# Two-layer MoE block on one core: SP's loads reordered, the first routing and its routed stage rescheduled, the low part of two slots on another engine

## The chip, the cores and the metric

One core of one Trainium2 chip. The metric is the device time of one launch in microseconds (us). The kernel before takes 1633.12 us, the median of three runs (1630.59 to 1636.07).

## What is computed

The reference takes x of 4 images of 512x512 and applies three residual steps:

```python
x = x + 0.5 * ffn(layernorm(x))      # mixture of experts
x = x + attn(layernorm(x))           # windowed attention, 16 channels
x = x + 0.5 * ffn(layernorm(x))      # the same mixture again

def ffn(x):
    shared = (silu(x @ sw1.T) * (x @ sw2.T)) @ sw3.T          # hidden 2048
    scores = sigmoid(x @ router_w.T)                          # 8 experts
    idx = top_k(scores + expert_bias, 2); w = scores[idx] / sum
    routed = sum over the two experts of w * expert(x)        # hidden 256 each
    return shared + routed
```

The attention looks at 8-token windows along rows for one half of the channels and along columns for the other, adds a depthwise convolution of v, projects, normalises and adds the residual.

## The kernel before

All five engines run programs written out by hand, synchronised by semaphores; each engine executes its own in order. Time is cut into *slots*. A slot is one 128-wide piece of the shared expert's hidden layer for one image of 512 rows: a gate product G and an up product U (12 matmuls each, L1253: each fp32 operand is split in a bf16 high and low part and three partial products are made), ScalarE's Silu of G (L1479), VectorE's multiply of U by it (L1634), ScalarE's bf16 high part of the result (L1489), the low part as fp32 minus high part (GpSimd, L1587), and the down product (12 matmuls, L1267) that accumulates in `psD`. TensorE does in slot s: G(s), U(s), then down(s-1). U(s) waits for the multiply of slot s-1, down(s-1) for the low part of slot s-1.

There are 128 slots: 16 for each image (UNIT), four images for the first mixture and four for the second. Around these, each engine's `slot(s)` fits in the rest of the work by tables:

- *Tiles* (`Prep`, 32): load 128 rows, statistics, norm (`vec_norm`, L382), store to `xnd`, transpose ("rows", L388), router logits (L408). `vec_norm` of tile n waits until the store of tile n-2 has landed.
- *Splits* (`SPLITS`): raw fp32 weights are loaded by SP (`load_raw`) and split into bf16 high (ScalarE, L257) and low (VectorE, L262) parts, eight shared chunks in slots -2 to 13 and eight experts after them. Shared chunks are stored and later reloaded by ScalarE's queue (`load_gu`, `load_down`).
- *Routing* (`route`, slots 14 to 17 for the first mixture): VectorE picks two experts of each token; TensorE computes the ranks (`pe_ranks`, L609) at position 3 of slot 15; lists of rows for each block are made in slots 18 and 19 (`vec_list`, `pe_list`, L639), indices in slot 21.
- *Constants of the attention*: loaded by ScalarE's queue from slot `CONST_SLOT` on; their product with the bias (`bias_product`) one slot ahead of `BIAS_SLOT`; VectorE does 18 small steps in slots `BIAS_SLOT` and the next three.
- *Routed stage* (`routed`): before slots `ROUTED_AT` = 24 and 116 every engine goes through 39 blocks of 128 gathered rows times the weights of one expert (L1355, L1372, L1385, L1397), about 187 us each. Slot 23's down product is flushed first. At its end GpSimd issues the gathers of the first three combine tiles, and then enters the slot.
- *Combine* (`Combine`, 16 tiles each time): GpSimd gathers two rows for each token (L555), SP loads the third (L561), VectorE sums (L576, L579), for the first four tiles it also makes statistics and norm (L591), SP stores (L567, L570). `COMBINE_SLOT` puts tiles 0, 1 in the slot behind the stage, then 2, then 3 and 4, then 5, then 6 and 7. Only then, in slots 35 to 39, tiles 8 to 15.
- *Halves* (`Half`, 8 units of the attention): SP loads a unit in 8 DMAs of 64 KB (`Half.sp_load`, L949), TensorE transposes it ("turn", L969, slots D-2) and projects it (L982), VectorE does softmax and products in pieces (`vec_work`, L1002, L1016, L1033) from slot D to slot B, then "back" and "proj" on TensorE, and in `NORM_SLOT` VectorE's `vec_spread` and `vec_finish` (L1112 to L1129), for which TensorE's "out" transposes wait (L1137). D is 29, 37, 46, 55, 64, 72, 81, 90. `spare` estimates the free VectorE time of a slot, and the pieces are put in by it.
- *Evacuations* (`Evac`): after 16 slots `psD` is added to the rows; image 1's first part is evacuated at the first routed stage (`EVACS`).

SP's order is what `slot(s)` in its block writes: prep loads, evacuation loads and stores, the combine's stores of this slot, the loads of the next slot's combine tiles, prep stores, weight stores and raw loads, then the units' loads. The first unit's load stands in slot 26 and the second's in slot 33.

## Time and profile before

| | us |
|---|---|
| median of three runs | 1633.12 |
| the profiled execution | 1636.73 |
| its span | 1634.7 |
| mean granted TensorE clock | 0.978 of full speed |

| engine | busy us | share |
|---|---|---|
| TensorE matmuls (PE) | 1536.6 | 94% |
| VectorE (DVE) | 997.5 | 61% |
| ScalarE (ACT) | 557.1 | 34% |
| GpSimd (POOL) | 503.6 | 31% |

The times are of one profiled execution. An engine's busy time counts only while it executes; waiting, and the issuing of a DMA, are idle. Idle time of an engine is listed with what ended it, for instance `[3.60 <-DVE rows L707]`: 3.60 us idle, ended by VectorE's instruction of line 707. "Granted clock" is the share of TensorE's full speed that the chip allowed (1.00 is 2.4 GHz, 0.50 is 1.2 GHz).

### The profile page before, as it was taken

How to read it: one execution, taken by the hardware profiler on the slowest of the kernel's cores; microseconds unless marked ns; L12 is line 12 of the kernel's file. 1: busy time of each engine (PE TensorE's matmuls, PEld its weight loads, DVE VectorE, ACT ScalarE, POOL GpSimd, SP SyncE). 2: the span in 40 equal slices, each digit the busy share in tenths (PEclk: the TensorE clock that was granted, in tenths of full speed). 3: DMA queues.
4: the chain of work that ended last, by engine and by line, in shares of the span. 5: the costliest groups of instructions: out<-in, count | busy, mean ns of one | idle time of the engine just before them, and what ended most of it. 6: DMA issues, size and time to landing. Idle time of an engine off the chain costs nothing.

```text
span 1634.7 us, 21706 instructions
## 1 busy us (share of the span) xinstructions
PE 1536.6 (94%) x7574; PEld 772.5 (47%) x7574; DVE 997.5 (61%) x1390; ACT 557.1 (34%) x1080; POOL 503.6 (31%) x424
## 2 busy tenths in 40 slices
PE   5999898999959798989998999999999999999999
PEld 3555344555424344535544554455445444555444
DVE  3665743444336788798779888888933543444333
ACT  3456222444312223333433433343322213444211
POOL 1321112222233555152434443252512112222253
PEclk9999999999979899999999999999999999999999
DMA  6887424333463675144423642264227234334485
GB/s 232 310 303 288 157 90 148 117 116 116 125 185 110 184 228 154 40 137 142 129 70 104 165 157 65 98 180 148 54 89 221 76 111 139 116 116 116 136 293 199
DMA packets 117465, 243.76 MB, mean 149 GB/s; under 512 B 15985, under 2 KB 40562, under 8 KB 113906
## 3 DMA queue, kind: packets, MB, share of 16 engines
q1 hardware_dynamic: 79632, 138.97, 25.1%
q10 hardware_dynamic: 26370, 66.17, 13.0%
q0 software_dynamic: 11360, 37.23, 7.8%
q8 instruction: 66, 1.08, 0.3%
q14 instruction: 37, 0.30, 0.1%
HBM read 168.39 MB, written 72.88 MB: 148 GB/s over the span
## 4 chain that ended last, share of the span: by engine, by line
PE 78%; DVE 11%; issue 4%; DMA 3%; POOL 1%; ACT 1%; SPq 1%; POOLq 0%; ACTq 0%; DVEq 0%
PE bank L1253 32%; PE bank L1267 15%; PE bank L1372 12%; PE bank L1397 6%; PE bank L982 3%; PE bank L1355 2%; DVE region L1002 2%; PE bank L1094 1%; PE bank L408 1%; PE bank L1385 1%; DMA rows<-sorted_y,slots 1%; DVE region L1016 1%; DVE stats L417 1%; PE bank L388 1%; DMA region<-xnd,idxs 1%
## 5 line engine op out<-in xcount | busy, mean ns | idle before, releaser
L1253 PE MATMUL bank<-xT,wb 128*128 128x512 bf16 x2688 | 620.2, 382 | 8.0 <-DVE wb L262 4.5
L1253 PEld LDWEIGHTS bank<-xT,wb 128*128 128x128 bf16 x2688 | 264.8, 99 | 322.1 <-issue 22.6
L1587 POOL TENSOR_TENSOR hs<-sgh,hs 128x512 bf16<-128x512 f32 x128 | 157.9, 1233 | 752.3 <-ACT hs L1489 752.2
L1267 PE MATMUL bank<-wb,hs 128*128 128x512 bf16 x1536 | 367.5, 384 | 4.2 <-POOL hs L1587 4.2
L1634 DVE TENSOR_TENSOR sgh<-bank,sgh 128x512 f32<-128x512 f32 x128 | 88.1, 688 | 274.5 <-PE bank L1253 273.5
L1267 PEld LDWEIGHTS bank<-wb,hs 128*128 128x128 bf16 x1536 | 151.4, 100 | 182.5 <-issue 12.0
L1372 PE MATMUL bank<-wr,region 128*128 x936 | 232.1, 385 | 0.0
L1489 ACT ACTIVATE hs<-sgh 128x512 bf16<-128x512 f32 x128 | 80.9, 632 | 331.0 <-DVE sgh L1634 327.1
L1002 DVE TENSOR_TENSOR region<-region 128x1024 f32<-128x1024 f32 x128 | 184.4, 1441 | 2.4
L1580 POOL DMA_INDIRECT region<-xnd,idxs x78 | 74.0, 949 | 257.5 <-PE bank L1355 256.0
L1479 ACT ACTIVATE sgh<-bank 128x512 f32<-128x512 f32 x128 | 76.3, 596 | 216.1 <-PE bank L1253 213.2
L1372 PEld LDWEIGHTS bank<-wr,region 128*128 128x128 bf16 x936 | 89.4, 99 | 78.9 <-issue 5.8
L1397 PE MATMUL bank<-wr,region 128*128 x468 | 113.7, 379 | 1.2 <-DVE region L1704 1.2
L1694 DVE TENSOR_TENSOR region<-bank,region 128x256 f32<-128x256 f32 x78 | 33.1, 424 | 105.6 <-ACT region L1521 105.6
L1687 DVE TENSOR_TENSOR region<-bank,region 128x512 bf16<-128x512 f32 x78 | 53.9, 691 | 58.4 <-ACT region L1515 58.2
L1521 ACT ACTIVATE region<-bank 128x256 f32<-128x256 f32 x78 | 29.9, 383 | 172.7 <-PE bank L1372 172.7
L555 POOL DMA_INDIRECT rows<-sorted_y,slots x64 | 64.9, 1014 | 74.1 <-issue 68.8
L1253 PE MATMUL bank<-region,wb 128*128 128x512 bf16 x384 | 85.3, 379 | 0.0
L1016 DVE TENSOR_REDUCE region<-region 128x128 f32<-128x1024 f32 x64 | 78.1, 1220 | 2.2
L1033 DVE TENSOR_REDUCE region<-region 128x128 f32<-128x1024 f32 x64 | 78.1, 1220 | 2.2
L1397 PEld LDWEIGHTS bank<-wr,region 128*128 128x128 bf16 x468 | 45.6, 98 | 56.3 <-issue 1.5
L576 DVE SCALAR_TENSOR_TENSOR rows<-rows,coef 128x512 f32<-128x512 f32 x32 | 29.5, 920 | 55.5 <-DMA rows<-x2p 32.2
(161 smaller groups left out, 1600.2 us busy)
## 6 DMA issues: line engine op xcount, KB each, us to landing
wb<-wsplit ACTq DMA_DIRECT2D x42, 1024.0 KB, 6.0
wb<-wsplit ACTq DMA_DIRECT2D x42, 512.0 KB, 4.0
sorted_y<-region SPq DMA_DIRECT2D x78, 256.0 KB, 2.0
wsplit<-wb SPq DMA_DIRECT2D x8, 1536.0 KB, 6.8
wr<-wall SPq DMA_DIRECT2D x6, 1536.0 KB, 7.7
rows<-x SPq DMA_DIRECT2D x32, 256.0 KB, 5.4
region<-wall SPq DMA_DIRECT2D x8, 1024.0 KB, 8.5
xnd<-rows SPq DMA_DIRECT2D x32, 256.0 KB, 2.8
```

The source lines that it names most:

```text
L1002: o.do(e.tensor_tensor(t, few.to_broadcast(full), many.to_broadcast(full), ALU.mult))
L1016: o.do(e.tensor_reduce(self.s[r][:, two], self.tmp.rearrange("p (n c) -> p n c", c=H), AX.X, ALU.add))
L1033: o.do(e.tensor_reduce(self.Q[r][:, two], self.tmp.rearrange("p (n b) -> p n b", b=WL), AX.X, ALU.add))
L1253: m = e.matmul(ps[:], wb[:, w % 2, wp, at:at + P], xt[:, xp, c, :], start=(i == 0), stop=(i == 3 * NDC - 1))
L1267: m = e.matmul(psD[tt][:], hs[:, s % 2, hp, tt * P:(tt + 1) * P], wb[:, w % 2, wp, at:at + D], start=(first and i == 0), stop=(last and i ...
L1372: m = e.matmul(psH[k % 2][:], xsT[k % 2][:, xp, c * P:(c + 1) * P], words_of(k, wp, c * D), start=(n == 0), stop=(n == 3 * NDC - 1))
L1397: m = e.matmul(psY[k % 2][:], hT[k % 2][:, hp, kt, :], words_of(k, wp, at), start=(n == 0), stop=(n == 3 * KT - 1))
L1479: e.activation(sgh[:, s % 2, :], psG[:], ACT.Silu).then_inc(S("h_silu").sem, 1)
L1489: e.activation(hs[:, s % 2, 0, :], sgh[:, s % 2, :], ACT.Copy).then_inc(S("h_hi").sem, 1)
L1580: e.indirect_dma_start(out=xs[k % RX], out_offset=None, in_=xnd, in_offset=bass.IndirectOffsetOnAxis(ap=idxs[:, k:k + 1], axis=0)).then_in ...
L1587: e.tensor_tensor(hs[:, s % 2, 1, :], sgh[:, s % 2, :], hs[:, s % 2, 0, :], ALU.subtract).then_inc(S("h_lo").sem, 1)
L1634: e.tensor_tensor(sgh[:, s % 2, :], psU[:], sgh[:, s % 2, :], ALU.mult).then_inc(S("h_mul").sem, 1)
```

## The change

- SP: expert 0's raw weights are loaded in the prologue behind the first two shared chunks, and experts 1 to 5 each two slots sooner; all experts' splits are two slots sooner, but the last's one slot later. The load of the first unit moves from slot 26 to slot 24, that of the second from slot 33 to slot 28.
- The first routed stage stands before slot 23 instead of 24. The combine tiles 0 to 7 and the evacuation at it move with it; `D_SLOT` stays.
- Constants are loaded one slot sooner, the bias product and VectorE's bias steps two slots sooner (slots 12 to 15). The first ranks product moves from slot 15, position 3 to slot 16, position 0.
- In slots 23 and 116 VectorE makes the low part, right behind its multiply, and GpSimd doesn't.
- `spare` takes 7.0 instead of 5.5 off a norm slot. Of the softmax pieces four move by it: half 4's `scores 1,1` from slot 66 to 65, half 5's `scores 1,0` from 74 to 75, half 7's `scores 1,2` from 92 to 93 and `values 0,0` from 93 to 94.

```diff
--- before.py
+++ after.py
@@ -83,7 +83,7 @@
     UNIT = NU * KT
     UNITS = 2 * IMAGES
     SLOTS_ALL = UNITS * UNIT
-    ROUTED_AT = (UNIT + 8, 7 * UNIT + 4)
+    ROUTED_AT = (UNIT + 7, 7 * UNIT + 4)
     assert W3OFF + KT * D == WW and NB == 39 and UNIT == 16 and NU == E and NT == 16
 
 
@@ -216,7 +216,7 @@
         for w in range(NU):
             SPLITS += [(2 * w - 2, "gu", w), (2 * w - 1, "down", w)]
         for ex in range(E):
-            at = 2 * ex + 4 if ex < E - 1 else UNIT + 3
+            at = 2 * ex + 2 if ex < E - 1 else UNIT + 4
             SPLITS += [(at, "gu", NU + ex), (at + 1, "down", NU + ex)]
         SPLITS.sort(key=lambda p: p[0])
         SPLIT_NO = {(kind, n): k for k, (_, kind, n) in enumerate(SPLITS)}
@@ -283,7 +283,7 @@
             if s % 2 == 0 and 0 <= s < 2 * (NU - 2):
                 return [s // 2 + 2]
             if s % 2 == 1 and 0 < s < 2 * (E - 2):
-                return [NU + s // 2]
+                return [NU + s // 2 + 1] if s // 2 + 1 < E - 2 else []
             return [NU + E - 2] if s == 2 * NU - 4 else [NU + E - 1] if s == 2 * NU - 2 else []
 
 
@@ -820,10 +820,11 @@
 
 
         HALF_MOVES = 16 * 8
-        BIAS_SLOT, BIAS_STEPS = UNIT - 2, (5, 5, 4, 4)
-        CONST_SLOT = 2
+        BIAS_SLOT, BIAS_STEPS = UNIT - 4, (5, 5, 4, 4)
+        CONST_SLOT = 1
         LOADED, STATS, NORMED, ROWS, LOGITS = range(5)
-        D_SLOT = [ROUTED_AT[0] + 5 + 35 * h // 4 for h in range(HALVES)]
+        D_SLOT = [ROUTED_AT[0] + 6 + 35 * h // 4 for h in range(HALVES)]
+        LOAD_SLOT = [ROUTED_AT[0] + 1, ROUTED_AT[0] + 5] + [d - 4 for d in D_SLOT[2:]]
         B_SLOT = D_SLOT[1:] + [D_SLOT[-1] + 8]
         NORM_SLOT = [b + 2 for b in B_SLOT[:-1]] + [B_SLOT[-1] + 2]
         OUT_AT = [((n + 1, 4), (n + 1, 5)) for n in NORM_SLOT]
@@ -850,7 +851,7 @@
 
         PIECES = [t[ROWS] + ("rows", n, 0) for n, t in enumerate(TILE)]
         PIECES += [t[LOGITS] + ("logits", n, 0) for n, t in enumerate(TILE)]
-        PIECES += [(ROUTE_SLOT[f] + 1, 3, "ranks", f, 0) for f in range(2)]
+        PIECES += [(ROUTE_SLOT[f] + 2 - f, 0 if f == 0 else 3, "ranks", f, 0) for f in range(2)]
         PIECES += [(LIST_SLOT[f] + 1 + k, 4, "list", f, k) for f in range(2) for k in range(2)]
         PIECES += [(BIAS_SLOT - 1, 5, "bias", 0, 0)]
         for h in range(HALVES):
@@ -885,7 +886,7 @@
 
             left = 7.5 - 0.8 + sum(PE_SHARE.get(p[2], 1.0) for p in PIECES if p[0] == s)
             left -= sum(2.2 * (t[STATS] == s) + 0.6 * (t[NORMED] == s) + 0.7 * (t[ROWS][0] == s) for t in TILE)
-            left -= 5.5 * (s in NORM_SLOT) + 2.8 * (s in EV_AT)
+            left -= 7.0 * (s in NORM_SLOT) + 2.8 * (s in EV_AT)
             left -= sum((1.5 + 2.0 * (m < TI)) * (at == s) for m, at in enumerate(COMBINE_SLOT))
             return max(left, 0.5)
 
@@ -1181,6 +1182,7 @@
                     Prep(n).sp_load(e)
                 load_raw(e, 0)
                 load_raw(e, 1)
+                load_raw(e, NU)
 
                 def slot(s):
                     for p in preps(s, LOADED):
@@ -1213,7 +1215,7 @@
                     for n in raws_at(s):
                         load_raw(e, n)
                     for h in range(HALVES):
-                        if s == D_SLOT[h] - (3 if h < 1 else 4):
+                        if s == LOAD_SLOT[h]:
                             Half(h).sp_load(e)
                         if s == B_SLOT[h]:
                             Half(h).sp_reload(e)
@@ -1582,7 +1584,7 @@
                                          ).then_inc(S(f"rows_gathered{k % RX}").sem, 16)
 
                 def slot(s):
-                    if s >= 0:
+                    if s >= 0 and s not in ROUTED_AT:
                         e.wait_ge(S("h_hi").sem, s + 1)
                         e.tensor_tensor(hs[:, s % 2, 1, :], sgh[:, s % 2, :], hs[:, s % 2, 0, :],
                                         ALU.subtract).then_inc(S("h_lo").sem, 1)
@@ -1632,6 +1634,10 @@
                         e.wait_ge(S("h_silu").sem, s + 1)
                         e.wait_ge(S("h_u").sem, s + 1)
                         e.tensor_tensor(sgh[:, s % 2, :], psU[:], sgh[:, s % 2, :], ALU.mult).then_inc(S("h_mul").sem, 1)
+                    if s in ROUTED_AT:
+                        e.wait_ge(S("h_hi").sem, s + 1)
+                        e.tensor_tensor(hs[:, s % 2, 1, :], sgh[:, s % 2, :], hs[:, s % 2, 0, :],
+                                        ALU.subtract).then_inc(S("h_lo").sem, 1)
                     for ev in evac_after(s):
                         ev.vec_sum(e, o)
                     for p in preps(s, NORMED):
```

## Rows read from the trace of the kernel before

**Rows 1.** The page: part 1 (busy by engine) and part 4 (the chain by engine).
```profile
PE 1536.6 (94%) x7574; PEld 772.5 (47%) x7574; DVE 997.5 (61%) x1390; ACT 557.1 (34%) x1080; POOL 503.6 (31%) x424
...
PE 78%; DVE 11%; issue 4%; DMA 3%; POOL 1%; ACT 1%; SPq 1%; POOLq 0%; ACTq 0%; DVEq 0%
```

**Rows 2.** Waits of TensorE: who waited for whom: us in total, times, longest us.
```profile
PE bank L969 <- DMA region<-xln: 26.5, 2, 17.5
PE bank L1137 <- DVE region L1129: 19.6, 5, 6.2
...
PE bank L1267 <- POOL hs L1587: 4.2, 5, 1.9
```

**Rows 3.** Chain at the head; one stretch: busy us by engine, clock, DMA, GB/s.
```profile
6.28 9.43 DMA xnd<-rows
...
29.23 11.87 PE bank L1253 x48
...
10.40:15.10 4.70, 2.93 (x13) 2.46 (x13) 1.03 (x3) 1.44 (x4) 0.55 (x1) 1.00 0.98 330
```

**Rows 4.** Timeline of TensorE over the first routing (start, us); one stretch.
```profile
168.81 0.76 PE L609 MATMUL bank<-rows,tri 128*128 128x128 f32 x2 [3.60 <-DVE rows L707]
...
188.99 5.34 PE L1253 MATMUL bank<-xT,wb 128*128 128x512 bf16 x24
...
196.76 2.75 PE L1253 MATMUL bank<-xT,wb 128*128 128x512 bf16 x12
201.64 4.35 PE L1253 MATMUL bank<-xT,wb 128*128 128x512 bf16 x12 [2.12 <-DVE sgh L1634]
...
219.73 1.20 PE L639 MATMUL bank<-rows 128*128 128x78 bf16 x16 [3.23 <-DVE rows L633]
...
165.20:236.30 71.10, 61.54 (x290) 28.08 (x290) 45.75 (x109) 15.77 (x22) 8.09 (x7) 0.93 0.36 124
```

**Rows 5.** Behind the first routed stage: chain, timeline, one stretch, instructions of L402.
```profile
448.81 1.47 PE L1267 MATMUL bank<-wb,hs 128*128 128x512 bf16 x6 [1.89 <-POOL hs L1587]
...
452.60 0.68 DVE sgh L1634
...
458.51 0.93 SPq L561 DMA_DIRECT2D rows<-x1p  x2
...
458.96 5.57 DMA rows<-sorted_y,slots
...
470.58 0.50 SPq L949
...
478.12 1.09 PE bank L969 x4
...
478.00:482.50 4.50, 4.38 (x15) 2.71 (x16) 0.00 (x0) 1.19 (x2) 0.00 (x0) 0.50 0.00 0
...
L402 DVE TENSOR_TENSOR xT<-rows,xT x20: 680/684/1622, 8.6 to 1145.0; 128x512 bf16<-128x512 f32 x20
```

**Rows 6.** Timeline of VectorE around the second unit's turn (slots 34, 35).
```profile
554.06 0.68 DVE L1634 TENSOR_TENSOR sgh<-bank,sgh 128x512 f32<-128x512 f32 x1
...
567.35 0.69 DVE L1634 TENSOR_TENSOR sgh<-bank,sgh 128x512 f32<-128x512 f32 x1 [7.71 <-PE bank L1253]
```

**Rows 7.** Timelines of VectorE and TensorE in norm slots 74 and 92.
```profile
972.86 2.55 DVE L1002 TENSOR_TENSOR region<-region 128x1024 f32<-128x1024 f32 x1
...
981.32 0.63 PE L1137 MATMUL bank<-ident,region 128*128 128x128 f32 x4 [0.88 <-DVE region L1129]
...
984.16 0.66 PE L1137 MATMUL bank<-ident,region 128*128 128x128 f32 x4 [0.92 <-ACT scores L413]
...
1156.58 0.63 PE L1137 MATMUL bank<-ident,region 128*128 128x128 f32 x4 [2.44 <-DVE region L1129]
```

**Rows 8.** Timelines of TensorE and VectorE behind the second routed stage, slot 123.
```profile
1589.21 5.13 PE L1253 MATMUL bank<-region,wb 128*128 128x512 bf16 x23
...
1591.05 0.68 DVE L1634 TENSOR_TENSOR sgh<-bank,sgh 128x512 f32<-128x512 f32 x1
```

## Prediction

> **What bounds the kernel now.** I read the page first, parts 1 and 4 [rows 1]: TensorE is busy 1536.6 of 1634.7 us and is 78% of the chain that ended last. So the time is TensorE's work plus its idle time, about 98 us, and a step is worth only what it takes out of that. Next the waits of TensorE [rows 2], which say where the idle time is: 26.5 us in two waits of the "turn" transposes for the load of a unit (L969), the longer 17.5; 19.6 us in five waits of the "out" transposes for VectorE's `vec_finish` (L1137); 4.2 us for GpSimd's low part (L1267), twice behind a routed stage. The chain and timelines of those places then say what comes late there, and what would be late next.
>
> In the stretches that the change touches TensorE runs in order: slot s is gate product, up product (needs the multiply of slot s-1, L1634), then the down product of slot s-1 (needs its low part). Starts of the up/gate group of neighbouring slots lie 7.77 us apart when nothing waits (at 188.99 and 196.76) [rows 4].
>
> **The change part by part**, each against the profiled execution.
>
> *Head: expert 0's raw weights loaded before everything else, a loss.* SP now issues 1.5 MB more behind `load_raw(e, 1)`, and all that SP issues later stands behind it. The chain [rows 3] shows what: the 256 KB store `xnd<-rows` of tile 0 was issued at 6.28 and landed 9.43 us later, because 3 MB of weights were ahead of it; `vec_norm` of tile 2 waits for it, and from there everything follows without slack to the first product at 29.23. The last raw weights crossed in 4.7 us at 330 GB/s, which is 1.5 MB. The same again: 4.7 us lost, one for one, with 1 us less or more as its bounds. Nothing behind absorbs it, as no wait of TensorE falls in slots 1 to 14. The earlier split of the experts (slots 2, 3) and the constants (slot 1) fall in slots like the ones that already carry them without a TensorE wait: nothing.
>
> *First routing.* Before, TensorE waits 3.60 (ranks), 2.12 (a multiply behind the ranks' sums) and 3.23 us (list), and after each its clock is granted at half: 12 matmuls then take 4.35 instead of 2.75 us [rows 4]. From 165.2 to 236.3 are 71.1 us for seven slots (54.4), the ranks (1.2) and two lists (1.5): 57.1 if nothing waits, so 14.0 are to be had. Is VectorE late next? The ranks in slot 16 are wanted a down product (2.6) and half a gate product (1.3) after 165.2, at 169.1; they were released at 168.81 and need the same VectorE work as before. The bias steps of slot 14 stay in front of its next multiply; I allow 0.3 for that. From slot 15 on VectorE loses bias steps and four splits; all it was busy with, 45.75 us, would fit into 57.1, and less is left. I take 13.7. Expert 14's weights are now wanted two slots sooner; the 1.5 MB of expert 13 no longer stand before them, so I take no wait, at worst 2 us; the low end is 10.
>
> *Low part on VectorE in slot 23, stage one slot sooner, first unit's load ahead of tiles 3 and 4.* These act together [rows 5]. Before, the slot behind the stage waits 1.89 us, because the low part is queued behind six gathers on GpSimd. VectorE makes it right behind its multiply, at the price of L402, 0.69 us (1.62 at worst), in front of a tile whose gathers it waits for anyway. So 1.89 is saved, but TensorE then wants the next up product 5.2 us (down, gate) after 446.9, at 452.1, and the multiply for it comes at 452.60. That multiply is behind the sums and norms of tiles 0 and 1, and the stage's move puts 1.5 MB of weight reloads into the time of their gathers; I add 1 us to them (0 to 3). The up product starts at 454.4, the saving is given back.
> From there down 2.6, one slot 7.77, half a gate product 1.3 and the rest of this slot 2.7: the turn is wanted at 468.8. The load: SP issued the rows of tiles 3 and 4 at 458.51 to 459.4; the unit's load now follows, 1.4 us later because of VectorE: 460.8. From first issue (470.58) to the turn (478.12) it took 7.5; with the gathers (5.57 here) and a reload beside it I add 2: 470.3. Against 478.12 that is 7.8 us sooner with one slot (7.77) more already done. Half clock until 482.5 cost 2 us and goes. Then tiles 3 and 4, hidden in the wait until now, make the next multiply about 1 us late. Sum 16.6; I take 16.5, ends 12 and 19. The second unit's load moves five slots ahead on SP, past the load and the stores of the evacuation of slot 32; those loads have two free slots and hide it.
>
> The Trainium skill, SBUF — State Buffer, "Who interferes with whom", says that VectorE instructions with two SBUF inputs and GpSimd instructions that read SBUF exclude each other for their whole length. By that rule the low part could also hold back a gather and what follows by up to its own length, and the sum would be 0.7 us less; the 0.69 and 1.62 of L402 are the same form without and with a neighbour.
>
> *Second unit's turn* [rows 6]. The wait is 9.0 us, but VectorE is behind here: the multiply of slot 34 is only at 554.06, so the up product of slot 35 can start at 554.8 and, with one qkv piece, end at 558.3; VectorE is done at 559.64 (567.35 less 7.71 idle). The next multiply is 7.7 us sooner. Then VectorE may wait for the gathers of tiles 8 and 9, which are issued only behind slot 34's low part and take some 5.6 each [rows 5]: I allow 1.4. Gain 6.3, ends 3.5 and 8.
>
> *Softmax pieces out of the norm slots* (7.0 for 5.5 in `spare`; by the formula it moves four, of halves 4, 5 and 7) [rows 7]. In slot 74 one piece (its product alone 2.55) stands before `vec_finish`; without it both waits (0.88 and 0.92) go: 1.8. In slot 92 the same piece goes and with it the wait of 2.44: 2.3. In slot 66 the piece only moves ahead of the multiply, the end of `vec_finish` comes 0.8 sooner. Sum 4.9, ends 2 and 5.5.
>
> *Low part on VectorE in slot 116* [rows 8]. 1.87 us go from the wait. But the multiply of slot 122 comes at 1591.05 + 0.68, and its up product starts at 1589.21 + 2.6: it is already just in time, and what paces it (load, sum and store of the combine, one behind the other) does not move. TensorE catches up with it. Gain 0.3, ends 0 and 1.9.
>
> Sum: -4.7 + 13.7 + 16.5 + 6.3 + 4.9 + 0.3 = 37.0. From the profiled 1636.7 that gives 1599.7; the median of the runs shown is 3.6 lower, 1633.1, which gives 1596.1. I forecast 1598 between them.
>
> **Rivals.** *DMA crowding at the first turn.* The unit's load is issued while gathers, rows and a weight reload of 1 MB are in flight. For it: a gather already took 5.57 us there. Against: the load's own last landing was the only thing that TensorE waited for, with nothing else behind it. If load and gathers come 4 us later each, the turn term falls by 8: 1606. 
> *VectorE takes over.* Where TensorE's wait goes, the multiply is late instead. I counted it at slots 25 and 35; if it also eats half of the routing's gain and of the second turn's: 1608.
> *A part doesn't act.* The bias product moves two slots ahead but the constants only one; if they land late, TensorE stands in slot 11. Before there were two slots between the last of them and the product and no wait, now one. At most a slot and a little, 9 us: 1607.
> *Slower.* One mechanism: crowding in slots 23 to 28 that passes into every step there, tiles 1, 2, 3-4, 5 and the unit's load, each of which feeds the next. It starts to cost more than all gains when each of the five comes over 7.4 us later (37.0 / 5), and reaches 1641 at 8.4 us. A gather took 5.57 at most in this chain, so its delay would have to grow far beyond anything shown.
>
> **Numbers.** Forecast (1591 to 1604) 0.57; crowding 0.14; VectorE takes over 0.11; constants 0.04; better than 1591 (tail and turn at their good ends) 0.09; under 5 us of gain by several at once 0.03; slower 0.02. All good ends give 45 us, all bad ends 23 us. The range 1587 to 1614 takes both in, on the median's scale. 0.3% is 4.9 us, about what a measurement of this kernel can tell from no change: faster 0.95, same 0.03, slower 0.02.
>
> **What would show it.** First product at about 34 instead of 29.2; no wait at L609 and L639 and no half clock between slots 14 and 22; L969 waits 0 to 4 us at the first unit and none at the second, with a new wait of L1253 for L1634 in slots 25 and 35; L1267 waits for no GpSimd; L1137 from 19.6 to about 14.5; in the tail a new wait of 1 to 2 us for a multiply. Wrong would be a head without loss, a first turn that still waits over 6 us, or list waits that stay.

## The result, and the profile after

The changed kernel takes **1596.99 us** (median of 4 runs, 1595.46 to 1599.15), the kernel before beside it 1633.84; the ratio is 0.9777, 95% interval 0.9756 to 0.9798. The forecast was 1598. With five more runs beside the last experiments, its nine times go from 1595.46 to 1602.10, median 1597.8. The profiled execution took 1599.15, 37.6 us less than the profiled one of before; it is the slowest of its four runs, 2.2 us above their median. One run of the kernel before (2302.37 us) and one of the kernel with the stage put back (8782.42 us) lie far outside all others, and every median and ratio here is of the other runs.

The page of the changed kernel, part 1 and the chain by engine, which answer to [rows 1]:

```profile
PE 1531.7 (96%) x7574; PEld 769.8 (48%) x7574; DVE 996.1 (62%) x1392; ACT 557.2 (35%) x1080; POOL 502.4 (31%) x422
...
PE 83%; DVE 7%; DMA 4%; issue 3%; POOL 2%; ACT 1%; SPq 0%; POOLq 0%; DVEq 0%; ACTq 0%
```

TensorE's busy time fell by only 4.9 us (fewer matmuls at half clock); the rest was idle time. Its waits, as in [rows 2]:

```profile
PE bank L388 <- DVE rows L382: 13.2, 3, 6.3
PE bank L1255 <- DVE sgh L1636: 11.4, 5, 4.4
PE bank L1138 <- DVE region L1130: 9.8, 2, 5.8
PE bank L1357 <- DMA region<-xnd,idxs: 8.5, 4, 2.9
...
PE bank L1082 <- DVE region L1047: 4.3, 1, 4.3
PE bank L970 <- DMA region<-xln: 2.4, 1, 2.4
...
PE bank L1269 <- POOL hs L1589: 0.5, 3, 0.2
```

The rows of the kernel before that two of them answer to, beside those of [rows 2]:

```profile
PE bank L1253 <- DVE sgh L1634: 3.6, 3, 2.1
PE bank L1081 <- DVE region L1046: 1.3, 1, 1.3
```

(Lines have moved: L1253 is now L1255, the up and gate product; L1267 now L1269, the down product; L1634 now L1636, the multiply; L969 now L970, the turn; L1137 now L1138, the "out" transposes; L1081 and L1046 now L1082 and L1047; GpSimd's low part L1587 now L1589, VectorE's is L1639.) The turns' 26.5 us are 2.4, "out" went from 19.6 to 9.8 (11.2 in a second trace of the same kernel), the ranks' and lists' waits are gone. In their place TensorE waits longer for the multiply (3.6 before, 11.4 now) and for the merge of a softmax (L1082, 1.3 before, 4.3 now), and at the head 3.0 us longer for the first norms (L388, 10.2 before, 13.2 now).

**Where the time went.** Multiplies of one slot can be set side by side in two traces. The start of the multiply of slot s before, less that after, is what has been gained up to there:

| slots | gained there, us | forecast | gained so far |
|---|---|---|---|
| head (slot 1) | -3.8 | -4.7 | -3.8 |
| first routing (to slot 22) | +14.6 | +13.7 | +10.8 |
| stage, first turn (to slot 33) | +12.6 | +16.5 | +23.4 |
| second turn (to slot 65) | +2.8 | +6.3 | +26.1 |
| norm slots 66, 74, 92 | +3.4, +2.2, +2.6 | +4.9 | +34.3 |
| second stage | +0.9 | - | +35.2 |
| tail (to slot 127) | +2.0 | +0.3 | +37.3 |

This table is what the text below calls the ledger. (Each entry is rounded by itself; the expectations wrote 14.7 for the routing and 8.1 for the norm slots.) The sum, 37.3, is almost the forecast's 37.0, but the terms are not: the two turns fell 7.5 us short, and the norm slots, the routing, the tail and the head made up for it. The experiments ask which of these differences are real.

The head and the turns in the changed kernel: from the chain of waits, the store of [rows 3]; from TensorE's timeline, the slots that answer to [rows 5] and the wait for the merge.

```profile
6.21 12.47 DMA xnd<-rows
...
437.42 5.30 PE L1255 MATMUL bank<-xT,wb 128*128 128x512 bf16 x12 [4.39 <-DVE sgh L1636]
...
456.88 0.63 PE L970 MATMUL bank<-ident,region 128*128 128x128 f32 x4 [2.38 <-DMA region<-xln]
...
562.14 0.96 PE L1082 MATMUL bank<-ident,region 128*128 128x128 f32 x4 [4.27 <-DVE region L1047]
```

The store lands 3.0 us later than before, and the first product starts at 32.20 instead of 29.23. The routing's slots now run at full clock, with 0.3 us of idle time: the stretch from 164.5 to the multiply of slot 22 (the columns are those of [rows 4])

```profile
164.50:225.60 61.10, 60.78 (x311) 28.32 (x310) 44.66 (x104) 13.54 (x22) 8.73 (x7) 1.00 0.43 152
```

### The profile page after: what moved, and what is told of

Same layout as the page of the kernel before. It is cut to its first block, busy times and chain, and to the rows that moved or that the text cites. A ratio compares the mean times of both kernels' runs of the same rounds, so it can differ in the third digit from the quotient of the medians.

```text
span 1597.4 us, 21707 instructions
## 1 busy us (share of the span) xinstructions
PE 1531.7 (96%) x7574; PEld 769.8 (48%) x7574; DVE 996.1 (62%) x1392; ACT 557.2 (35%) x1080; POOL 502.4 (31%) x422
## 4 chain that ended last, share of the span: by engine, by line
PE 83%; DVE 7%; DMA 4%; issue 3%; POOL 2%; ACT 1%; SPq 0%; POOLq 0%; DVEq 0%; ACTq 0%
PE bank L1255 36%; PE bank L1269 17%; PE bank L1374 13%; PE bank L1399 6%; PE bank L983 2%; PE bank L1357 2%; PE bank L1095 2%; PE bank L408 2%; DMA rows<-sorted_y,slots 1%; PE bank L1387 1%; DVE region L1003 1%; PE bank L388 1%; DMA xnd<-rows 1%; DMA region<-xnd,idxs 1%; DVE stats L417 1%
## 5 line engine op out<-in xcount | busy, mean ns | idle before, releaser
L1255 PE MATMUL bank<-xT,wb 128*128 128x512 bf16 x2688 | 622.6, 383 | 15.9 <-DVE sgh L1636 11.4
L1255 PEld LDWEIGHTS bank<-xT,wb 128*128 128x128 bf16 x2688 | 264.9, 99 | 331.7 <-issue 25.5
L1589 POOL TENSOR_TENSOR hs<-sgh,hs 128x512 bf16<-128x512 f32 x126 | 154.5, 1226 | 708.1 <-ACT hs L1491 708.1
L1269 PE MATMUL bank<-wb,hs 128*128 128x512 bf16 x1536 | 365.7, 382 | 0.5 <-POOL hs L1589 0.5
L1269 PEld LDWEIGHTS bank<-wb,hs 128*128 128x128 bf16 x1536 | 151.2, 100 | 177.6 <-issue 10.6
L1636 DVE TENSOR_TENSOR sgh<-bank,sgh 128x512 f32<-128x512 f32 x128 | 88.1, 689 | 217.9 <-PE bank L1255 216.6
L1255 PE MATMUL bank<-region,wb 128*128 128x512 bf16 x384 | 85.3, 379 | 0.0
```

What stands on the lines that cost most here:

```text
L1255: m = e.matmul(ps[:], wb[:, w % 2, wp, at:at + P], xt[:, xp, c, :], start=(i == 0), stop=(i == 3 * NDC - 1))
L1269: m = e.matmul(psD[tt][:], hs[:, s % 2, hp, tt * P:(tt + 1) * P], wb[:, w % 2, wp, at:at + D], start=(first and i == 0), stop=(last and i ...
L1589: e.tensor_tensor(hs[:, s % 2, 1, :], sgh[:, s % 2, :], hs[:, s % 2, 0, :], ALU.subtract).then_inc(S("h_lo").sem, 1)
L1636: e.tensor_tensor(sgh[:, s % 2, :], psU[:], sgh[:, s % 2, :], ALU.mult).then_inc(S("h_mul").sem, 1)
```

## The experiments

All start from the changed kernel, the last one from the kernel before it. Two values are given for each: the median of its 4 or 5 runs with its ratio to the kernel before beside it, to be held against 0.9777, and what its trace shows slot by slot against the first trace of the changed kernel. The second is the finer one, as it tells in which slot time goes or comes, but it compares two single executions, and since that trace is of a run 2.2 us above its median, gains against it tend to come out high and losses low. Where medians and traces differ by more than that, both are given.

**The same kernel again.** No edit.

> The changed kernel once more, unaltered, beside the others of this call: how far two executions of one program differ at each slot, and so how small a step the comparisons can carry. Expected: multiplies of the same slot within 1 us of the first trace up to the stage, 1 to 2 us behind the two routed stages, where the gathers' waits differ; median 1595 to 1599.

Median 1601.75 us (1596.33 to 1602.10), ratio 0.9797 (0.9775 to 0.9820): above the 1595 to 1599 that was expected. The multiply of slot 25 lies 1.1 us before that of the first trace, those of slots 28, 38 and 127 lie 0.9, 2.4 and 2.8 us behind; 1 to 2 was expected. Most of the 1.5 us between slots 28 and 38 is one event, a longer wait for the merge (4.27 in the first trace):

```profile
456.25 1.09 PE L970 MATMUL bank<-ident,region 128*128 128x128 f32 x4 [2.55 <-DMA region<-xln]
...
564.00 1.09 PE L1082 MATMUL bank<-ident,region 128*128 128x128 f32 x4 [6.12 <-DVE region L1047]
```

In the nine traces with this order of loads at the head the multiply of slot 0 comes between 39.5 and 41.0 us. So a term can't be read better than to 1 us, across the second turn not better than to 2; and the medians of one kernel in two sessions differ by 4.8 us.

**Head.** Expert 0's raw weights are loaded in slot -1.

```
...
                 load_raw(e, 1)
-                load_raw(e, NU)
...
         def raws_at(s):
+            if s == -1:
+                return [NU]
```

> Base is the changed kernel; only the load of expert 0's raw weights moves, from ahead of everything to SP's slot -1, behind the stores and row loads of tiles 0 to 3. It is the clean price of the head term. Theory (the 1.5 MB stand ahead of the 256 KB stores that the norms wait for): the first product comes at about 29.2 instead of 32.2, multiply 1 some 3.8 us sooner, everything behind keeps its distance, 1593.2 us against 1597.0. Rival (the head is paced by the splits of raw weights 0 and 1 and would come out the same): 1597. A second rival: expert 0 lands too late for its split in slot 2, and a wait of some us appears at slot 3 or 4: 1597 to 1600.

Median 1595.55 us, ratio 0.9778 (0.9759 to 0.9796). The medians alone would say that nothing changed. The trace's chain has the store again at its length of before, and the first product at 29.35:

```profile
6.35 9.48 DMA xnd<-rows
```

Its multiplies are 3.4 us sooner from slot 0 to slot 22, 3.5 to 4.0 from slot 29 to the second stage and 4.6 at the end. In the five traces without the load ahead of the tiles the multiply of slot 0 comes between 36.0 and 36.8 us, in the nine with it between 39.5 and 41.0. No wait of TensorE appears in slots 2 to 4. The head's price is shown by the traces, though the medians differ by only 1.4 us, and it was needless: the load has room behind the tiles.

**First routing.** Head and first routing as before.

```
-            at = 2 * ex + 2 if ex < E - 1 else UNIT + 4
+            at = 2 * ex + 4 if ex < E - 1 else UNIT + 3
...
-        BIAS_SLOT, BIAS_STEPS = UNIT - 4, (5, 5, 4, 4)
-        CONST_SLOT = 1
+        BIAS_SLOT, BIAS_STEPS = UNIT - 2, (5, 5, 4, 4)
+        CONST_SLOT = 2
...
-        PIECES += [(ROUTE_SLOT[f] + 2 - f, 0 if f == 0 else 3, "ranks", f, 0) for f in range(2)]
+        PIECES += [(ROUTE_SLOT[f] + 1, 3, "ranks", f, 0) for f in range(2)]
```

(and `load_raw` of the experts where it was.)

> Base is the changed kernel; the head and the first routing are as before the change (expert 0 loaded in slot 1 and split in slot 4, bias steps from slot 14, constants from slot 2, ranks behind the gate product's half of slot 15), all else as changed. Theory (the terms add, head -3.8 and routing +14.7): the first product is back at 29.2, the waits for ranks and list and their half clock return between slots 15 and 22, the stage starts some 10.8 us later than in the changed kernel: 1608. Rival (the routing's gain needs the stage's move or the low part too, since the last split and the lists lie two slots before the stage): more than 14.7 lost, 1612 or above, with a wait at the stage's start.

Median 1610.61 us, ratio 0.9867 (0.9847 to 0.9888), 13.6 us above the changed kernel; its trace ends 10.0 us later. The old waits are back with their old lengths:

```profile
PE bank L639 <- DVE rows L633: 3.8, 2, 3.2
PE bank L609 <- DVE rows L707: 3.6, 1, 3.6
```

Its multiplies are 3.7 us sooner up to slot 14 and 11.1 later at slot 22: 14.7 for the routing, as in the ledger. At slot 23, behind the stage, 10.2 are left; the stretch from the multiply in front of this stage to the one behind it takes 196.2 to 197.6 us in the fourteen traces, so the 0.9 between them is no part of the routing. It adds to the rest, as the theory had it.

**The first turn**, in three runs. The unit's load back in slot 26:

```
-        LOAD_SLOT = [ROUTED_AT[0] + 1, ROUTED_AT[0] + 5] + [d - 4 for d in D_SLOT[2:]]
+        LOAD_SLOT = [ROUTED_AT[0] + 3, ROUTED_AT[0] + 5] + [d - 4 for d in D_SLOT[2:]]
```

> Base is the changed kernel; the first unit's load goes back from slot 24 to slot 26, behind the stores of tiles 3 and 4. Forecast's arithmetic: the load is then issued after the combine of tiles 3 and 4 as before the change, some 8 to 12 us later than 443.6, and lands about that much later, while the turn is wanted at the same time: TensorE's wait at the turn grows from 2.4 to about 10, the time to 1605. Rival (crowding: with the load out of their way the gathers of tiles 3 and 4 come about 3 us sooner and the load itself is back at 7.5 us from first issue to last landing): the wait grows to 5 or 6 only, 1600.

Median 1615.47 us, ratio 0.9896 (0.9880 to 0.9912), 18.5 us above the changed kernel: dearer than either theory had it. SP's timeline and TensorE's:

```profile
462.73 0.95 SPq L561 DMA_DIRECT2D rows<-x1p  x2
463.80 3.75 SPq L950 DMA_DIRECT2D region<-xln  x8
...
472.05 1.08 PE L970 MATMUL bank<-ident,region 128*128 128x128 f32 x4 [16.30 <-DMA region<-xln]
```

SP issues the load 20 us later than the 443.63 of the changed kernel, because in slot 26 the sum of tile 5 and the loads of the tiles behind it stand before it too. I had counted 8 to 12. By the trace 16.7 us are lost at slot 33. Taking off the 1.2 us that this trace's head is late, the load's place alone is worth 15.5 us.

The stage back before slot 24:

```
-    ROUTED_AT = (UNIT + 7, 7 * UNIT + 4)
+    ROUTED_AT = (UNIT + 8, 7 * UNIT + 4)
...
-        D_SLOT = [ROUTED_AT[0] + 6 + 35 * h // 4 for h in range(HALVES)]
-        LOAD_SLOT = [ROUTED_AT[0] + 1, ROUTED_AT[0] + 5] + [d - 4 for d in D_SLOT[2:]]
+        D_SLOT = [ROUTED_AT[0] + 5 + 35 * h // 4 for h in range(HALVES)]
+        LOAD_SLOT = [ROUTED_AT[0] + 1, ROUTED_AT[0] + 4] + [d - 4 for d in D_SLOT[2:]]
```

> Base is the changed kernel; only the first routed stage goes back from slot 23 to slot 24, with combine, first unit's load and low part keeping their distance to it and the halves' slots kept where they are. Forecast's arithmetic (nothing but one slot less between the stage and the turn): 7.8 us less to hide the load, 1605. Rival (the stage's move is what put the 1 MB reload of slot 23 beside the gathers of tiles 1 and 2; here it is issued ahead of the stage): the gathers of tiles 1 and 2 take 4 to 5.5 us instead of 6 to 8, TensorE's wait behind the first combine falls from 4.4 to 1 to 2 us, and only half of the slot is lost, 1600 to 1602.

Median 1604.85 us, ratio 0.9831 (0.9813 to 0.9848).

```profile
442.37 2.76 PE L1255 MATMUL bank<-xT,wb 128*128 128x512 bf16 x12 [1.92 <-DVE sgh L1636]
...
460.21 1.08 PE L970 MATMUL bank<-ident,region 128*128 128x128 f32 x4 [11.19 <-DMA region<-xln]
```

The wait behind the first sums is 1.9 us instead of 4.4, the turn's 11.2 instead of 2.4. Slot 28 comes 4.6 us later and not 7.8; behind the second turn it is 6.3, the difference being again the longer wait for the merge (6.12 for 4.27). The rival's mechanism shows in the trace, but its time (1600 to 1602) came out too low: the median is 7.9 us above the changed kernel's, which is the forecast's arithmetic (1605). How much of the slot the crowding gives back is therefore open.

GpSimd makes the low part of slot 23 again:

```
-                    if s >= 0 and s not in ROUTED_AT:
+                    if s >= 0 and s != ROUTED_AT[1]:
```

(and the other way round on VectorE.)

> Base is the changed kernel; only the low part of slot 23 is GpSimd's again, behind the issues of the six gathers. Forecast's arithmetic: TensorE waits some 1.9 us for it in slot 24, but the multiply of slot 24 is paced by the gathers of tiles 1 and 2 and comes when it comes, so its wait of 4.4 us in slot 25 shrinks by the same: no change within 0.5 us, 1597. Rival (each wait counts for itself, as the low part of slot 116 did with 4.1 us where 0.3 was expected; a half clock behind the first wait would add to it): 1.9 to 4 us slower, 1599 to 1601.

Median 1599.03 us, ratio 0.9797 (0.9778 to 0.9815), beside 1601.75 for the changed kernel in the same session.

```profile
428.75 2.76 PE L1269 MATMUL bank<-wb,hs 128*128 128x512 bf16 x12 [1.47 <-issue]
...
436.09 2.76 PE L1255 MATMUL bank<-xT,wb 128*128 128x512 bf16 x12 [1.99 <-DVE sgh L1636]
...
454.82 1.09 PE L970 MATMUL bank<-ident,region 128*128 128x128 f32 x4 [4.31 <-DMA region<-xln]
```

1.47 us of waiting come back before the down product (the profile names no releaser; GpSimd's low part, behind the last gather, runs from 427.53 to 428.69), and the wait for the multiply is shorter by more (1.99; 4.39 and 3.46 in the two traces of the changed kernel). At slot 28 the three are within 0.9 us. By the traces this part of the change gives nothing, as the forecast argued. The medians don't decide it: this run is 2.0 us slower than the changed kernel in its first session and 2.7 faster than in its last.

**Crowding.** ScalarE issues the 1 MB reloads of slots 23, 25 and 35 a slot later.

```
+        HELD = (ROUTED_AT[0], ROUTED_AT[0] + 2, 2 * UNIT + 3)
...
-                        if reload_after(s):
+                        if reload_after(s) and s not in HELD:
                             load_gu(e, s)
+                        if s - 1 in HELD:
+                            load_gu(e, s - 1)
```

> Base is the changed kernel; ScalarE issues the 1 MB gate and up reloads of slots 23, 25 and 35 one slot later, so that they don't lie beside the gathers of tiles 1, 2, 3, 4 and 9 and beside the first unit's load. Theory (crowding of these transfers is what both turns fell short by): gathers of tiles 1 and 2 take 4 to 5.5 us again instead of 6 to 8, TensorE's wait in slot 25 falls from 4.4 to 1 to 2, the turn wait from 2.4 to 0 to 2, and the merge before slot 38 comes 1 to 2 sooner: together 3 to 7 us, 1590 to 1594. Rival (the gathers are slow by themselves or VectorE's own order sets the pace): no change, 1597. Risk that would show as a new wait of TensorE for its weights at slot 26 or 28: the held reload of slot 23 has only some 9 us before it is wanted; then 1597 to 1602.

Median 1594.30 us, ratio 0.9764 (0.9748 to 0.9780), 2.7 us below the changed kernel and just above the theory's range; by the trace, which is of the fastest of its runs (1591.47), 7.1 to 7.6 us sooner from slot 36 to the second stage. So that it gains is shown, how much is not settled: 3 us by the medians, 7 by the traces. The DMA views of the two kernels over the same stretch behind the stage (issues: KB of one, median us from issue to landing), changed kernel first:

```profile
wb<-wsplit ACTq DMA_DIRECT2D x1, 1024.0 KB, 8.8
...
rows<-sorted_y,slots POOLq DMA_INDIRECT x6, 6.5
```

```profile
rows<-sorted_y,slots POOLq DMA_INDIRECT x6, 4.2
```

The same six gathers take 4.2 us without the megabyte beside them and 6.5 with it. VectorE's wait for the gathers of tile 1 shows what hung on it: 4.02 us in the changed kernel, none here, so the multiply of slot 24 starts 9.9 us behind that of slot 23 and not 13.9 (13.0 to 15.0 in the eight traces whose programs are alike between slots 22 and 24, 9.8 again in the run below with the reload held):

```profile
432.65 0.75 DVE L576 SCALAR_TENSOR_TENSOR rows<-rows,coef 128x512 f32<-128x512 f32 x1 [4.02 <-DMA rows<-sorted_y,slots]
```

```profile
432.71 0.69 DVE L1640 TENSOR_TENSOR sgh<-bank,sgh 128x512 f32<-128x512 f32 x1
```

TensorE's wait for that multiply goes, the turn's falls from 2.38 to 1.06 us, the merge's from 4.27 to 3.65. New are 1.69 us in slot 28 for a copy of ScalarE and 0.5 us for the held weights, the small end of the risk. The unit's eight DMAs still took 7.1 us in the median, so the megabyte is only a part of what slowed them. VectorE waited 8.73 us for the gathers of tile 5, beside which the held reload of slot 25 now lies, and 5.0 of the 7.7 us gained by slot 26 were lost again until slot 27.

**The second turn**, in two runs. The second unit's load back in slot 33 (`ROUTED_AT[0] + 5` in `LOAD_SLOT` becomes `D_SLOT[1] - 4`):

> Base is the changed kernel; the second unit's load goes back from slot 28 to slot 33, behind the load and the stores of slot 32's evacuation. It prices the second turn's term by itself. By the ledger of the two traces (2.8 us net at slots 35 to 38): the wait at the second turn returns, and the work behind it is no longer late, so the time goes up by 3 us to 1600. By the forecast's arithmetic, 6.3 us: 1603. Rival: the wait at the turn returns in full (9.0 us) while the wait of slot 38 for the merge stays, since VectorE's work there is longer than TensorE's either way: 1604 to 1606.

Median 1602.88 us (1598.69 to 1604.32), ratio 0.9813 (0.9792 to 0.9833).

```profile
535.28 1.09 PE L970 MATMUL bank<-ident,region 128*128 128x128 f32 x4 [8.04 <-DMA region<-xln]
...
565.36 0.63 PE L1082 MATMUL bank<-ident,region 128*128 128x128 f32 x4 [1.32 <-DVE region L1047]
```

The turn's wait of 8.0 us is back, the merge's shrinks from 4.27 to 1.32, and the wait for the multiply of slot 34, 2.78 us, goes. At slot 41 only 1.1 us of loss are left (1.9 less 0.8 from the head), between slots 68 and 115 0.4, and against the second trace of the changed kernel, with its longer wait for the merge, none. The medians say 5.9 against the changed kernel's first session and 1.1 against its last. What is shown is that most of the turn's wait had been turned into two waits for VectorE; what the earlier load is worth, nothing or up to 6 us, is open.

The combine of tiles 8 to 15 two slots later:

```
-        COMBINE_SLOT += [2 * UNIT + 3 + 2 * (m // 3) + m % 3 // 2 for m in range(8)]
+        COMBINE_SLOT += [2 * UNIT + 5 + 2 * (m // 3) + m % 3 // 2 for m in range(8)]
```

> Base is the changed kernel; the combine of tiles 8 to 15 starts in slot 37 instead of 35. It tests what became the limit once the second turn no longer waits. Theory (VectorE: 3.7 us of waits for the gathers of tiles 8 and 9 and 4.5 us of their sums stand ahead of half 0's last softmax work, whose merge TensorE waits for at 562 us, 4.3 us and then half clock): the multiply of slot 36 comes right behind its up product, the merge wait of slot 38 shrinks to 0 to 1, and the half clock behind it goes: 4 to 6 us faster, 1591 to 1593, less what the same sums cost in slots 37 to 41 (0 to 3). Rival (the merge is late because of the softmax work itself): the wait stays at 3 us or more, 1596 to 1597.

Median 1592.03 us, ratio 0.9754 (0.9729 to 0.9778), 5.0 us below the changed kernel and inside the theory's range; by the trace 8.0 us sooner from slot 41. VectorE's timeline in the changed kernel, slot 35, and then TensorE's of this one where the merge's wait stood:

```profile
538.41 1.80 DVE L576 SCALAR_TENSOR_TENSOR rows<-rows,coef 128x512 f32<-128x512 f32 x1 [1.10 <-DMA rows<-sorted_y,slots]
...
543.56 0.75 DVE L576 SCALAR_TENSOR_TENSOR rows<-rows,coef 128x512 f32<-128x512 f32 x1 [2.56 <-DMA rows<-sorted_y,slots]
```

```profile
552.04 1.46 PE L1269 MATMUL bank<-wb,hs 128*128 128x512 bf16 x6
553.33 0.60 PE L1082 MATMUL bank<-ident,region 128*128 128x128 f32 x4
```

The wait is gone and so is the half clock behind it (12 matmuls in 2 x 1.46 us with the transposes between them). Some 4 of the 8 us are there already at slot 34: `spare` counts the combine, so the softmax pieces moved too, and the waits for the multiplies of slots 33 and 34 went as well; therefore the trace's gain is above the theory's range, and the run doesn't price the combine's place by itself. At slot 38 the gain is 10.5; of this 2.4 are lost again by slot 41, where the "out" transposes now wait 6.20 us for VectorE (4.01 in the changed kernel). VectorE was the bound there.

**Norm slots and tail.** The weight of a norm slot is 5.5 again, and the low part of slot 116 is GpSimd's.

```
-            left -= 7.0 * (s in NORM_SLOT) + 2.8 * (s in EV_AT)
+            left -= 5.5 * (s in NORM_SLOT) + 2.8 * (s in EV_AT)
...
-                    if s >= 0 and s not in ROUTED_AT:
+                    if s >= 0 and s != ROUTED_AT[0]:
```

(and the other way round on VectorE.)

> Base is the changed kernel; two parts far from each other are undone together: the weight of a norm slot is 5.5 again (four softmax pieces back into slots 66, 74, 92 and 94), and the low part of slot 116 is GpSimd's again. Read by stretches of the trace. Norm slots: by the ledger 3.4 us at slot 66, 2.1 at slot 74 and 2.6 at slot 92, 8.1 in all; by the forecast 0.8, 1.8 and 2.3, 4.9 in all. Tail: by the ledger 2.0 us, the whole wait of 1.87; by the forecast 0.3, because the combine would pace it. Sum by the ledger 10.1: 1607; by the forecast 5.2: 1602.

Median 1609.32 us, ratio 0.9855 (0.9833 to 0.9878). By the trace the loss grows by 1.2 us at slot 66, 1.2 at slot 74 and 2.6 at slot 92, 5.0 in all: the forecast's 4.9, not the ledger's 8.2. In the tail it grows by 4.0.

```profile
1518.98 4.04 PE L1269 MATMUL bank<-wb,hs 128*128 128x512 bf16 x12 [2.18 <-POOL hs L1589]
...
1521.70:1523.70 2.00, 2.00 (x7) 0.64 (x5) 1.20 (x1) 0.63 (x1) 1.15 (x1) 0.50 0.61 170
```

2.2 us of it are the wait, the rest half clock behind it (12 matmuls take 4.04 us, 2.76 in the same place before, where the wait was 1.87 and the clock stayed full). From slot 118 to the end every slot of this run takes 7.77 us: nothing but TensorE paces them. The median, 12.3 us above the changed kernel's, holds both parts and a longer wait for the merge (6.12 us).

**A version that beats both.** Head, held reloads and later combine together:

> Base is the changed kernel with three edits at once: expert 0's load behind the first tiles (4 us in the trace by itself), the reloads of slots 23, 25 and 35 held one slot (7.7), the combine of tiles 8 to 15 two slots later (8). If each acts where it was measured, they add except at the second turn, where the last two take out the same wait for the gather of tile 9 (about 2): the first product at 29.2, neither the wait for the multiply of slot 24 nor the merge's wait of slot 38, the trace's last multiply 16 to 18 us sooner, 1581 to 1584 by the median. Rival (the combine's transfers collide with what lies in slots 37 to 41 once all is sooner, or the later combine and the held reload cost each other's gain): 1587 or more.

Median **1582.39 us** (1580.72 to 1584.35), ratio 0.9696 (0.9677 to 0.9714). The last multiply is 18.5 us sooner than in the first trace of the changed kernel, and by the traces the edits add up (4.0 + 7.7 + 8.0 less some 2 that the last two share). By the medians the three give 1.4, 2.7 and 5.0 us alone and 14.6 together (19.4 against the changed kernel of the same session). Neither the wait for the multiply of slot 24 nor the one for the merge is left; the waits for multiplies and for the turn are now:

```profile
PE bank L1258 <- DVE sgh L1641: 3.6, 3, 2.9
PE bank L974 <- DMA region<-xln: 1.9, 1, 1.9
```

Instead the "out" transposes of slot 40 wait 5.15 us for VectorE (4.01 in the changed kernel).

And tiles 5 to 7 a slot later (`+ (m > 4)` in the first `COMBINE_SLOT`):

> The three edits of the run before, and the combine of tiles 5, 6 and 7 one slot later. With the reload of slot 25 held, its 1 MB lay beside the gathers of tile 5: one of them took 8.6 us, VectorE waited 8.7 for it, and 5 of the 7.7 us gained by slot 26 were lost until slot 28. Theory (that is crowding again, and tile 5 is not urgent): the multiply of slot 26 comes right behind its up product, TensorE's wait of 1.7 us in slot 28 for a copy of ScalarE goes, 3 to 5 us below the run before, 1577 to 1580. Rival (tiles 5 to 7 only carry the same wait one slot on, in front of the evacuation of slot 32, which needs them): 0 to 1 us of difference.

Median **1580.85 us** (1580.15 to 1582.62), ratio 0.9685 (0.9666 to 0.9703). At slot 24 this trace is 2.9 us behind the one before it, at slot 28 it is 1.8 ahead, at slot 29 0.6 behind: the wait in front of the multiply of slot 26 goes, and most of it is lost one slot on. Between slots 24 and 41 it gains 1.2 us, the median 1.5: the theory's 3 to 5 us didn't come, and the rival's 0 to 1 is nearer.

## Why the prediction was right, and where its steps were not

*Head.* -4.7 was forecast, -3.8 came, -3.4 by the experiment up to the first stage. The mechanism held (store 12.47 instead of 9.43 us); 1.5 MB cost 3.0 us on the store and 0.8 behind it, where the first 48 matmuls took 12.70 instead of 11.87 us, not 4.7 in one piece. They start at half pace, 0.40 us each where 0.22 is full, and keep it for the first 11 instead of the first 7; the profile's row for these stretches reads a granted clock of 1.00 all the same, so the clock is not shown as the cause.

*First routing.* 13.7 forecast; 14.6 in the ledger, 14.7 by the experiment. No wait of TensorE appeared in slot 11, so the constants' rival fell, and "VectorE takes over" did not show here.

*First turn.* 16.5 forecast, 12.6 measured, 12.0 in the second trace. The arrival that the forecast counted step by step failed in the two allowances for crowding. For the gathers of tiles 1 and 2 it added 1 us: the next multiply comes 13.90 us behind the stage's first one instead of 10.75, which is 3.1 (2.2 in the second trace). For the unit's load it added 2 us to 7.5: from its first issue (443.63) to the turn (456.88) it took 13.25, which is 5.7, and it was issued 1.9 us later than forecast. So the turn came 5.6 us later than forecast. TensorE still waited only 2.38 us there, because it was itself late behind that multiply, and 1.7 us were made good behind the turn. The gathers behind the stage took 6.5 us instead of the 4.2 with the reload held, and the eight DMAs of the unit 9.3 in the median, beside this 1 MB reload (5.1 in the run with the load back in slot 26, with no such reload beside them, and 4.3 before):

```profile
wb<-wsplit ACTq DMA_DIRECT2D x1, 1024.0 KB, 11.6
...
region<-xln SPq DMA_DIRECT2D x8, 64.0 KB, 9.3
```

That is the crowding rival in kind, at about half the size that I had given it (4 us of 8). The third of the rate that it spoke of did not come: 9.3 is 1.8 to 2.2 times the 5.1 and 4.3. The rule of the Trainium skill that I cited for it, "Queues, rings and completion order" in DMA: Bandwidth & Descriptors (an engine serves its queue rows in turn), fits these numbers; the trace shows the delay, not the turns. "The saving is given back" for the low part of slot 23 was right. Of the three edits that act together the low part carries nothing; undone alone, the load's place costs 15.5 us and the stage's 4.6 by the traces (18.5 and 7.9 by the medians), more together than the 12.6 that they gave, so they overlap and can't be priced as a sum.

*Second turn.* 6.3 forecast, 2.8 in the ledger, 0.9 in the second trace. The step that failed is the end of the sum: I followed VectorE to the multiply of slot 35 and stopped. Behind it the merge was already waited for in the profile of before, 1.3 us at L1081, in a row that I had not used (shown above); the merge stands in slot 37, and the expectations count it to slot 38, whose multiply it delays. A wait of 1.3 us after one of 9.0 says that VectorE is level with TensorE; whatever the turn gives back comes due there. This is "VectorE takes over", and by the two traces it took 3.5 to 5.4 of 6.3 us at the second turn. With the combine later both waits for VectorE were gone, so the lost time could be had.

*Norm slots.* 4.9 forecast and 5.0 measured by undoing them; the ledger's 8.2 holds 3 us that are no part of this edit. Slot 66 shows where from. VectorE's and GpSimd's timelines, kernel before and then the run with the pieces back, at the same instructions:

```profile
888.90 2.55 DVE L1002 TENSOR_TENSOR region<-region 128x1024 f32<-128x1024 f32 x1
...
888.89 1.48 POOL L1064 TENSOR_TENSOR region<-region,cw 128x512 f32<-128x512 f32 x1
```

```profile
864.95 1.21 DVE L1003 TENSOR_TENSOR region<-region 128x1024 f32<-128x1024 f32 x1
...
864.94 2.57 POOL L1065 TENSOR_TENSOR region<-region,cw 128x512 f32<-128x512 f32 x1
```

Two instructions that start within 0.01 us: in one run VectorE's takes 1.34 us longer, in the other GpSimd's 1.09. VectorE's is in front of `vec_finish`, for which TensorE waits 6.16 us in the one and 4.99 in the other. The rest of the 2.2 us at slot 66 is the half clock behind that wait: from the first "out" transpose to the next down product it takes 9.87 us in the one and 8.85 in the other, 7.37 where the clock stayed full (the run with the second unit's load back). Slot 74 repeats it: the same two instructions start 0.01 us apart, VectorE's takes 2.55 us before and 1.21 in the run with the pieces back, GpSimd's 1.48 and 2.59, and TensorE's wait of 0.88 us is only in the kernel before. That is nearly all of the other 1.0 us. The forecast had credited the edit with those 0.88 us.

*Tail.* 0.3 forecast, 2.0 in the ledger, 4.0 by undoing it, above my upper end of 1.9. The step that failed: "what paces it does not move". No wait for a multiply appeared, and in the kernel before as in the changed one and in this run the slots from 118 to 127 take 7.75 to 7.77 us on average, and TensorE waits nowhere in them for more than 0.16 us: it paced the tail all along, and VectorE's multiply of slot 122, "just in time", was no limit. The loads of the combine are issued slot by slot, which would let it move with the slots; no run tests that. The 4.0 of undoing it is a wait of 2.18 with half clock behind it, the ledger's 2.0 one of 1.87 without.

So the time was right within 1 us since misses of 7.5 us one way and 7.8 the other cancelled. That TensorE's waits could be taken out, and where, was right; the range, 1587 to 1614, was made for misses of single terms (its bad ends add up to 21.8 us of gain, not 23, which doesn't change it); the point was luck.

## What to carry to other kernels

When a wait is taken away, follow the engine behind it as far as the next place where it is waited for, and read even the small waits there: they show where two engines are already level. A transfer that is moved or left beside small urgent ones costs through them, so look at what else each queue issues in the same microseconds; here three megabyte reloads held back for one slot, a load issued behind the first tiles and a combine two slots later were worth another 15 to 19 us (medians of two sessions). And price a part by undoing it alone as well as by the difference of two traces: the two disagreed by 2 to 3 us in the norm slots and the tail.

## What the runs showed of the hardware

- In two places (norm slots 66 and 74) an instruction of VectorE with two inputs in SBUF and one of GpSimd start 0.01 us apart, and one of the two takes longer: VectorE's 2.55 for 1.21 us in the kernel before, GpSimd's 2.57 and 2.59 for 1.48 us in the run with the pieces back. The Trainium skill, SBUF — State Buffer, "Who interferes with whom", says that such a VectorE instruction contends with a GpSimd instruction that reads SBUF; that whoever issues first gets the shared ports for the whole instruction it says of VectorE's two-port modes. The trace's lengths agree (1.34 more beside one of 1.48, 1.09 more beside one of 1.21); which came first can't be read from the starts in the trace, since GpSimd's is 0.01 us ahead in all four.
- Whether half clock follows a wait is not settled by the wait's length: behind the turn's wait of 2.38 us the clock stayed full in one trace of the changed kernel, behind 2.55 us in the other it was half, and the first four transposes took 0.63 and 1.09 us. In front of the up product of slot 67 TensorE waits 2.91 to 2.92 us in twelve traces; in six of them the clock behind it was granted at half, in five at full, and in one it fell on the way.
- That half clock cost nothing: TensorE waits for VectorE's `vec_finish` right behind it, 0 to 1.4 us where the clock was half and 2.7 where it was full, and the multiply of slot 68 follows that of slot 65 by 31.7 to 31.8 us in all twelve. Half clock is no loss where another engine sets the pace, as VectorE does there.
- A wait for VectorE alone repeats from kernel to kernel (5.78 to 5.81 us for the first "out" transposes of slot 49 in every trace from the changed kernel on) unless a half clock shortens it, as in slot 67. What hangs on gathers varies: the multiply of slot 24 comes 13.0 to 15.0 us behind that of slot 23 in the eight traces whose programs are alike between slots 22 and 24. The first kind can be read from one trace, the second can't.
